# A fused macaron block on one core: a quarter of the keys' transpose ahead of the hidden units', and two moves inside a step in the first and last blocks

## What is computed

```python
x = x + 0.5 * ffn(layernorm(x))            # called A
x = x + attention(layernorm(x))            # called B
x = x + 0.5 * ffn(layernorm(x))            # called C
# ffn: gate, up = x @ Wgu.T ; h = silu(gate) * up ; rms_norm(h) @ Wp.T
```

## Time and profile before

| | us |
|---|---|
| runs shown | 2029.28, 2030.42, 2033.40 |
| the profiled execution | 2029.52 |
| its span, first to last instruction | 2027.6 |
| PE busy with matmuls | 1889.7 (93%) |
| VectorE / ScalarE busy | 1555.3 (77%) / 1499.2 (74%) |
| GpSimd busy | 576.8 (28%) |
| the 16 DMA engines, mean share of the transposes' queue | 77% |

### The profile page before, as it was taken

One profiled execution on the slowest core, in us unless ns is written; L12 is line 12 of the kernel. 1 busy time (PEld: TensorE's weight loads), 2 busy tenths in 40 slices (PEclk: granted clock), 3 DMA queues, 4 the chain that ended last, 5 costly groups with the idle time before them and its releaser, 6 DMA issues. The chain is left out here.

```text
span 2027.6 us, 37731 instructions
## 1 busy us (share of the span) xinstructions
PE 1889.7 (93%) x12447; PEld 913.0 (45%) x12688; DVE 1555.3 (77%) x4079; ACT 1499.2 (74%) x2871; POOL 576.8 (28%) x559
## 2 busy tenths in 40 slices
PE   6677799999999999999999999999999999999777
PEld 3353344444444444444444444444444444444333
DVE  8966787778787888778787878777887878777763
ACT  7836777777876877777876777777777787777762
POOL 2011333322332333222333332233333232222210
PEclk8888999999999999999999999999999999999989
DMA  7334788778986898878886898788887888878862
GB/s 234 121 64 94 140 150 160 135 138 157 156 153 121 146 163 150 141 143 154 156 143 130 149 161 152 142 142 151 158 145 129 150 157 154 146 128 148 140 116 62
DMA packets 1032673, 287.83 MB, mean 142 GB/s; under 512 B 1017120, under 2 KB 1018144, under 8 KB 1031968
## 3 DMA queue, kind: packets, MB, share of 16 engines
q1 hardware_dynamic: 1032480, 285.41, 77.1%
HBM read 25.17 MB, written 8.39 MB: 17 GB/s over the span
## 5 line engine op out<-in xcount | busy, mean ns | idle before, releaser
L731 ACT ACTIVATE masked<-masked,exp_bias,exp_scale 128x256 f32<-128x256 f32 (+1 forms) x1024 | 503.7, 562 | 8.6
L1103 PE MATMUL ps_yy<-wp_t,ht 128*128 128x512 bf16 x1991 | 479.9, 383 | 28.1 <-DMA ht<-hh 26.7
L1058 PE MATMUL ps_gu<-wgu_t,xt_A 128*128 128x512 bf16 x1941 | 469.0, 383 | 16.6 <-DMA xt_A<-xh 3.7
L1058 PE MATMUL ps_gu<-wgu_t,xt_C 128*128 128x512 bf16 x1944 | 463.1, 380 | 11.5 <-DMA xt_C<-xh 3.5
L860 DVE TENSOR_TENSOR prob<-masked,prob 128x1024 f16<-128x1024 f32 (+1 forms) x256 | 287.2, 1122 | 48.0 <-ACT prob L749 47.7
L1103 PEld LDWEIGHTS ps_yy<-wp_t,ht 128*128 128x128 f16 x2016 | 187.6, 98 | 264.9 <-issue 31.9
L554 POOL TENSOR_TENSOR xh<-xhat,xh 128x512 f16<-128x512 f32 x94 | 109.0, 1160 | 691.9 <-ACT xh L615 691.9
L1058 PEld LDWEIGHTS ps_gu<-wgu_t,xt_A 128*128 128x128 f16 x2048 | 192.1, 98 | 230.1 <-issue 11.7
L1058 PEld LDWEIGHTS ps_gu<-wgu_t,xt_C 128*128 128x128 f16 x2048 | 190.7, 97 | 219.9 <-issue 3.9
L875 DVE SCALAR_TENSOR_TENSOR hid<-ps_gu,h_scale_u,hid 128x512 f32<-128x512 f32 x252 | 189.1, 751 | 121.2 <-PE ps_gu L1058 118.4
L615 ACT ACTIVATE hh<-hid 128x512 f16<-128x512 f32 x256 | 160.6, 627 | 152.5 <-DVE hid L875 145.3
(11 more groups left out here) (165 smaller groups left out, 2261.6 us busy)
## 6 DMA issues: line engine op xcount, KB each, us to landing
stream<-in_L_attn_x_dram SPq DMA_DIRECT2D x32, 256.0 KB, 3.3
pt<-prob SPq DMA_TRANSPOSE x512, 3.3
out_dram<-stream SPq DMA_DIRECT2D x32, 256.0 KB, 2.4
prob<-in_L_ffn_w_gate_up_dram SPq DMA_DIRECT2D x4, 1024.0 KB, 5.5
ht<-hh SPq DMA_TRANSPOSE x256, 3.2
stream<-in_L_ffn_w_gate_up_dram SPq DMA_DIRECT2D x3, 1024.0 KB, 5.4
stream<-in_L_ffn_w_proj_dram SPq DMA_DIRECT2D x2, 1024.0 KB, 5.2
prob<-in_L_ffn_w_proj_dram SPq DMA_DIRECT2D x2, 1024.0 KB, 4.8
```

Source lines behind the costliest of these rows:

```text
L731: t = act.activation(p, p, ACT.Exp, bias=exp_bias[:, 4 * g + h:4 * g + h + 1], scale=exp_scale[:, 0:1])
L1058: t = pe.matmul(bank[:, :], xt[s][:, part, k, :], wgu_t[:, k, at:at + CH], start=(k == 0 and part == 0), stop=(k == KD - 1 and part == 1))
L1103: t = pe.matmul(ps_y[:, :], ht[:, n % HRING, i, :], wp_t[:, 4 * c + i % 4, :], start=(c == 0 and i == 0), stop=(c == NC - 1 and i == 2 * N ...
```

## The change

There are four edits. `light(step)` is true for steps 0 to 31 and from 248 on.

1. SP: `hidden_t` of a step moves from the end of the step to the beginning of the next one. Between two steps that leaves its place as it was, except that the store and the load of the old step now stand ahead of it. In front of it, in the step of a block's keys, stands now the first part (a quarter) of the keys' transpose, with its waits; the second part follows it.
2. SP: the keys' transpose stands ahead of the queries' (they are in different steps).
3. ScalarE: in light steps the tokens' high part is made ahead of `tanh_half` and the exponentials instead of behind them.
4. VectorE: in light steps B's statistics are made one step earlier (8b+5), at once behind `add_ffn` of A, instead of behind `gated` in 8b+6. This concerns blocks 1, 2, 3 and 31.

```diff
+        def light(step):
+            return step < 8 * 4 or step >= 8 * LAST
 # SP
             for step in range(FIRST_STEP, STEPS + 2):
+                def keys_t(b, part):
+                    pairs = (slice(0, 4), slice(4, HEADS // 2))[part]
+                    transpose(kt[:, pairs, b % BPS, :],
+                              k4[:, 2 * pairs.start:2 * pairs.stop, :, :].rearrange("p a b c -> p (a b c)"), t_k[part])
+                b = block_at(step, K_AT + 1)
+                if b is not None:
+                    sp.wait_ge(a_k, b + 1)
+                    sp.wait_ge(d_k, b + 1)
+                    need(sp, p_s, 16 * (b - 2))
+                    keys_t(b, 0)
+                s, b, c = ffn_at(step - 1)
+                if s:
+                    hidden_t(s, b, c, place(step - 1))
+                b = block_at(step, K_AT + 1)
+                if b is not None:
+                    keys_t(b, 1)
                 b = block_at(step, Q_AT + 1)
...
-                b = block_at(step, K_AT + 1)
-                if b is not None:
-                    sp.wait_ge(a_k, b + 1)
-                    sp.wait_ge(d_k, b + 1)
-                    need(sp, p_s, 16 * (b - 2))
-                    for part, pairs in enumerate((slice(0, 4), slice(4, HEADS // 2))):
-                        transpose(kt[:, pairs, b % BPS, :],
-                                  k4[:, 2 * pairs.start:2 * pairs.stop, :, :].rearrange("p a b c -> p (a b c)"),
-                                  t_k[part])
...
-                s, b, c = ffn_at(step)
-                if s:
-                    hidden_t(s, b, c, place(step))
                 b = complete("C", step, 4)
 # ScalarE
+                def tokens_hi():
+                    for s, offset in SPLITS:
+                        b = block_at(step, offset)
+                        if b is not None and in_steps(s, b) and not (s == "B" and b == 0):
+                            split_free(act, step, s)
+                            copy(xh[:, 0, :], xhat[:, :], g_xh[s], b + 1, a_xh[s])
+                if light(step):
+                    tokens_hi()
                 s, b, c, n = gate_at(step)
...
-                for s, offset in SPLITS:
-                    b = block_at(step, offset)
-                    if b is not None and in_steps(s, b) and not (s == "B" and b == 0):
-                        split_free(act, step, s)
-                        copy(xh[:, 0, :], xhat[:, :], g_xh[s], b + 1, a_xh[s])
+                if not light(step):
+                    tokens_hi()
 # VectorE
                 b = block_at(step, LN_B)
-                if b is not None and b > 0:
+                if b is not None and not light(step):
                     norm_stats("B", b, d_x1, b + 1)
...
                 b = complete("A", step, 2)
                 if b is not None:
                     add_ffn("A", b, d_x1)
+                b = block_at(step, LN_B - 1)
+                if b is not None and b > 0 and light(step):
+                    norm_stats("B", b, d_x1, b + 1)
```

## The result

The changed kernel takes **2044.29 us** (median of five runs, 2039.39 to 2046.91), the kernel before, run five times beside it, 2033.4: 1.0057 times as long, 95% interval 1.0043 to 1.0072. It is slower by 11 us. The forecast was 2025.4, with a range of 2013 to 2037; sign and size were wrong. The profiled execution took 2044.03, its span 2042.0 against 2027.6.

A forecast was written before the change was run, and what follows sets the result against it. PE was taken to bound the middle without slack, with stops to win at both ends. Keys +1.5, store and load +5, first blocks -7 and last blocks -4.5 gave -5 and 2025.4 us, range 2013 to 2037.

The forecast's parts named there:

- 1. The keys: Middle blocks: with a quarter of the keys ahead of `ht`, PE's wait moves from keys to `ht`; +1.5 us.
- The typical block: Middle, block 10 as example: wait moved from the keys to `ht` and not removed; -0.1 to +0.2 us.
- with the latencies as they are: Keys in blocks 4 to 30: the sum with the trace's `ht` latencies, +5 us; with 3.0 it was -4.
- 2. Store and load: Middle, step 8b+3: `ht` issued 1.1 us later behind store and load, landing after 3.6; +5 us, bounds +1 and +10.
- the bound of +10: Upper bound for store and load in the middle, keeping each block's own `ht` latency, up to 5.0 us.
- 3. First blocks: Start of the kernel: earlier `xh` and B's statistics remove PE stops and restore clock; -7 us, bounds -9.5 and -2.5.
- The stop of 2.94: First blocks, PE waiting for `xh` of A2: `xh` made at 155.8 and landed at 160.8, the stop goes to zero.
- +1, which a stop of the same length behind it absorbs: Block 0: its key quarter now waits for the keys in front of `ht`, costing 1 us that a later stop absorbs.
- 4. Last blocks: End of the kernel: earlier `xt_C` and exponentials shorten PE stops, against a later output projection; -4.5 us, bounds -7 and 0.
- The 1.24 and 2.22: Last blocks: PE stops that go because `xt_C` of blocks 29 and 30 comes some 2.4 and 3.6 us earlier.
- about half of it stays: Last blocks: the keys' stop of 2.92 us ends sooner, but `down` behind it waits for `ht`; about half remains.
- SP's order costs more than the ends give: Rival: late `ht` makes PE wait in the middle, +10 and +5, ends give only -2.5 and -4.5; 2038 us, chance 0.15.

The follow-up runs named there:

- the quarter alone: Kernel before with only the first quarter of the keys' transpose moved ahead of `ht`, store and load staying behind it: 2041.07 us, ratio 1.0041.
- the half: Kernel before with half of the keys (256 KB) instead of a quarter ahead of `ht`, store and load staying behind it: 2037.51 us, ratio 1.0027.

## Why the prediction was wrong

What bounds the kernel was read right: every stop of PE in the middle came through to the end, and landings followed issues. By the terms of the sum:

**1. The keys: +1.5 taken, about +9 measured** (-10.5 + 19.6; the quarter alone had +8, the half +6). The typical block was right, -0.1 to +0.2 against +0.1. The step that failed is the one that chose among latencies. I had the sum "with the latencies as they are" at +5 and took less, since "what stands behind a short transfer should be nearer to the least". It was not: `ht` of 8b+2 took 3.31 before and 3.28 behind the short part. And +5 was no upper bound, because a reorder moves the long landings. Before, the three of them fell in blocks that already stood still for late keys (6, 8, 28) and so would have cost little more; in the six other kernels that keep this part of SP's order they came again in 6 and 28, and in five of the six in 8. In the changed kernel they fell on blocks 10, 16, 19 and 29, at 1.1 to 2.2 each. For a transfer that moves to another place in the list, a long landing has to be priced for every block, not replayed.

**2. Store and load: +5 taken, +11.8 measured** (+6.6 alone). The order of things was right, and the size hung on one number: 3.6 for `ht` behind the load, from `xt_A`. It was 4.0 to 4.1. `xt_A` was issued as close behind the load as `ht` is now (a median gap of 0.17, against 0.10), so the neighbour looked fit; what the difference of 0.4 is made of, the runs don't settle. With a margin that ends at zero, 0.4 us decides: this was the bound of +10 kept for "up to 5.0", and it was the likely case. Here each block's own latency was the right thing to keep: all six of this `ht` that took over 3.9 before are among the ten longest after.

**3. First blocks: -7 taken, -3 measured**; -8.4, -8.5 and -6.4 in the three kernels with both ends' edits that keep `ht` in its old place there, one profile each. The stop of 2.94 went, `xh` came at 155.71 and `up` at 160.89, as worked out. The projection of queries came at 174.98, not 172.7 (5.1 for one landing). The failed step is "+1, which a stop of the same length behind it absorbs": I charged SP's order in the first blocks with the key quarter of block 0 alone. It also makes the `ht` of the next steps late, where PE waits already, and longer stops cost clock as well. Crediting the statistics with most of the gain was wrong too: alone they gave nothing, and ScalarE's edit alone -7.5 of the -8.4.

**4. Last blocks: -4.5 taken, -5.0 measured.** The stops of the earlier trace rows in the changed kernel:

```profile
1899.20 4.16 PE L1101 MATMUL ps_gu<-wo,ot 128*128 128x512 f16 x12 [2.91 <-issue]
...
1929.15 1.89 PE L1076 MATMUL ps_gu<-wgu_t,xt_C 128*128 128x512 bf16 x8
...
1931.95 0.39 PE L1111 MATMUL ps_s<-kt,qt 48*128 48x256 f16 x4 [0.91 <-DMA kt<-k]
...
1933.92 1.90 PE L1121 MATMUL ps_yy<-wp_t,ht 128*128 128x512 bf16 x8 [1.37 <-DMA ht<-hh]
...
1977.41 1.89 PE L1076 MATMUL ps_gu<-wgu_t,xt_C 128*128 128x512 bf16 x8
```

The 1.24 and 2.22 are gone, the 2.92 at the keys became 0.91 and 1.37 at `down` behind it ("about half of it stays": 2.28 of 2.92, more than half), the output projection waits 0.9 longer (2.03 to 2.91; 1.4 was reckoned before the pay-back).

**The sum.** 9.1 + 11.8 + 1.4 - 3.0 - 5.0 = +14.3, against the 14.4 by which the span grew. The rival "SP's order costs more than the ends give" was the true one. Its point of decision was rightly named, over 4 us for `ht` behind the load, but it was given 0.15. It also held both bounds, +10 and +5, as its price, and their sum with the ends' lower values would have been 2038; the measured terms pass both bounds. The two errors have one root: for each uncertain latency a value near the friendly end was taken, in a kernel with no slack on PE, where the cost of a late landing is one-sided.

## What to carry to other kernels

When a queue of transfers is reordered to bring one forward, list for each transfer that is pushed back how early it lands before it is needed, block by block, and compare this margin with the longest landings in the trace and not with the median. A margin of 1.2 us that looks idle was absorbing landings of over 4; take the place in the queue from a transfer that has more in hand, as the low half of the probabilities had. If some landings are long, look in the DMA records for what they have in common, and see whether the same ones come again. And time every edit of a bundle by itself: here one half was worth -13 us and the other +23.

## What the runs showed of the hardware

- A DMA transpose issued from SP delays the next one by its issue of about 1.3 us, whether it moves 128 KB or 256 KB; the next one's own time from issue to landing did not change (medians of 3.31 us before, 3.28 behind 128 KB, 3.30 behind 256 KB).
- Behind a store and a load of 256 KB each, issued within 1.1 us, a transpose landed in 3.96 to 4.09 (median) instead of 3.15; behind one of them in 3.35 and 3.47.
- The transpose `ht` takes 3.0 to 3.6 us mostly and up to 5 in one case of six (32 of 195 before). All of the long ones had a packet of the `instruction` queues under way between issue and landing; without one none took over 3.7 in ten kernels, unless it stood behind a store and a load. That the packet is the cause was not tested.
- With stops of PE of over 2 us in 21 of 27 blocks the granted clock fell behind them, to 0.72 in the window shown, and longer products added some 31 us to 58 us of stops. Behind a stop of 0.39, block 11's, `down` took its 1.90 as before.
